# A chain of four conditional layers on one core: scores once, by query, and probabilities turned by a transposing DMA

## The chip, the cores and the metric

One core of one Trainium2 chip. Its engines are TensorE (PE, matmuls), VectorE (DVE), ScalarE (ACT), GpSimd (POOL) and SyncE (SP, which here only issues DMAs). Each engine runs its own list of instructions in order; semaphores tie the lists together. The metric is the time on the device in microseconds (us), lower is better.

## The reference

Sixteen independent batch elements, each x of 256 tokens by 256 features in float32, go through four layers, each added to its input:

```python
x = x + einsum('bnh,boh->bno', x, W[subject]) + b[subject]        # a linear layer chosen per element
x = x + zX*laplace_x(x) + zY*laplace_y(x) + zR*x*(1-x)            # a stencil
# attention: 16 heads of 16; query = side + b_self, keys = x + b_prev (masked by length) and one
# further score per query, its own: s_self = q . k(side); softmax over 256 + 1 scores
x = x + (softmax([q k^T, s_self] * SCALE) @ [v ; v_self]) @ Wo + bo
# three experts, relu(x @ wi) @ wo with hidden 1024: one chosen by label and two shared,
# mixed by a softmax gate that is computed from token 0
x = x + eo*w0 + s0*w1 + s1*w2
```

The attention's numbers have to be near float32, so the kernel splits operands into parts: float32 products are made of three matmuls (hi*hi, hi*lo, lo*hi), and query and key heads are laid out as bfloat16 bands (three parts each, six products, stacked to 96 rows, with the mask as one row more).

## The kernel before

Everything of one element fits in the on-chip memory; the loop runs over elements. Five written order lists (PE_BODY, ACT_BODY, DVE_BODY, POOL_BODY, SP_BODY) say in which order each engine makes the stages of one turn. A turn works on three elements at once: `lag(name)` gives 0 for the preparation of element i (x1, q, lap, kp, vp and so on), 1 for the attention of element i-1, 2 for the experts (H0 to H11, P0 to P11) and the gate of element i-2. Lists with OPEN_ in front stand ahead of the loop, those with CLOSE_ behind it; the loop makes 14 turns. In the opening there are no experts yet, and PE makes matmuls without use (`fill`) between stages; the opening's lists name 132 of them, the closing's list 5.

**Experts.** H_s (line 859) makes 256 hidden columns in one PSUM bank out of 12 matmuls, each 128x128 by 256 columns. ACT takes relu into `hid_hi` (1160), DVE the rest into `hid_lo` (1391); P_s (886) multiplies on into two output banks. Two hidden banks and two buffers alternate.

**Preparation.** x1, q, ks, vs, kp, vp are the same sort of 12-matmul product into one of two front banks. All users of the front banks take them in turns (`RING`, `open_bank` at 752): a stage waits until the user two places before it is freed. q and k parts are rewritten by SP into `q_rows` and `k_rows` (`place`, 527: 6 DMAs each, those of `kp` at 589 and `k3` at 601), which the scores of the next turn read.

**Attention of one head h, before.** S_h (826): two matmuls give scores with the query on the partitions; DVE reduces them to their maximum (1294) and frees the bank. After heads 0 to 7 and 8 to 15, `top0` and `top1` (1295) take the larger of that and the own score, and split it into three bfloat16 parts; `m0` and `m1` turn these on PE (835), ACT copies them to SBUF (1102), and SP writes them as three further rows of `q_rows` (604). E_h (841) then makes the scores a second time, with the key on the partitions and the maximum already subtracted by these rows; ACT makes two exps of 512 columns out of PSUM, one in float32 and one in float16 (1117, 1121; head 11's float16 one is a cast on DVE, 1313), DVE (seven heads) or POOL (nine heads) subtracts them into `prob_lo` (1314, 1607). `attend` (780) multiplies both parts with the values, eight matmuls of 49 columns, three heads behind E_h and between its two matmuls. Heads 0 to 7 fill `pv` first; `half` (1316) sums them, and POOL's `norm` (1593) divides. `att` (1328) does the same for heads 8 to 15 on DVE, after which PE turns the result (`aT`, 912) and multiplies by Wo. `m1` on POOL (1588) weighs the own values by `p_self`.

**Queues.** SP issues, in the order of SP_BODY, the pieces of the chosen expert's weights (`wo0`.., `wi_load`), the placements, the next element's inputs (`load`) and the store (`sum`). Each waits at the head of the queue for what it needs.

## Time and profile before

| | |
|---|---|
| Median of 3 runs (lowest to highest) | 1002.27 us (998.57 to 1002.36) |
| Profiled execution: its own time, its span | 998.3 us, 995.7 us |
| TensorE clock granted, mean | 0.997 |
| PE busy | 972.3 us, 98% of the span, 9659 matmuls |
| DVE, ACT, POOL busy | 796.9 (80%), 686.8 (69%), 635.9 us (64%) |
| DMA | 82.71 MB, 28% of 16 engines |
| Chain that ended last | PE 75%, POOL 9%, issue 8% |

Busy time is the union over an engine's instructions. PE's matmuls overlap each other, so the duration of one (about 0.28 us) is more than what it costs; the cost is the distance from its start to the next start. The chain view follows the last instruction back to what released it.

### The profile page before, as it was taken

What the parts mean: (1) busy time and instruction counts of PE and PEld (TensorE: products, weight loads), DVE (VectorE), ACT (ScalarE), POOL (GpSimd) and SP (SyncE); (2) the same over time, 40 slices, a digit from 0 to 9 for tenths busy, and PEclk for the clock granted to TensorE, in tenths of its full rate; (3) what the DMA queues carried; (4) which work ended last, traced back from release to release, by engine and by line L of the source; (5) the groups of instructions that cost most, each with busy time, mean ns of one, the idle gap of its engine ahead of it and who ended that gap; (6) DMA issues with size and microseconds to landing.
All of it is one profiled execution on the core that took longest, in us unless ns stands there. A gap on an engine that the chain in (4) does not pass through costs nothing.

```text
span 995.7 us, 28043 instructions
## 1 busy us (share of the span) xinstructions
PE 972.3 (98%) x9659; PEld 932.9 (94%) x9659; DVE 796.9 (80%) x1566; ACT 686.8 (69%) x1442; POOL 635.9 (64%) x544
## 2 busy tenths in 40 slices
PE   7889999999999999999999999999999999999997
...
DMA packets 92029, 82.71 MB, mean 83 GB/s; under 512 B 12100, under 2 KB 90980, under 8 KB 92004
## 3 DMA queue, kind: packets, MB, share of 16 engines
q1 hardware_dynamic: 91572, 81.99, 28.2%
q10 hardware_dynamic: 432, 0.39, 0.1%
q8 instruction: 15, 0.25, 0.1%
...
## 4 chain that ended last, share of the span: by engine, by line
PE 75%; POOL 9%; issue 8%; DVE 3%; ACT 3%; SPq 1%; DMA 1%; POOLq 0%; ACTq 0%; DVEq 0%
PE out L721 8%; PE out L722 8%; PE hid L721 8%; PE out L723 8%; PE hid L722 7%; PE hid L723 7%; PE front L847 4%; PE front L833 4%; PE front L721 4%; PE front L723 3%; PE front L722 3%; POOL prob_lo L1607 3%; POOL exp_lo L1543 2%; PE pv L788 2%; PE pv L789 2%
## 5 line engine op out<-in xcount | busy, mean ns | idle before, releaser
L721 PE MATMUL hid<-x_hi,exp_hi 128*128 128x256 f32 x768 | 230.6, 300 | 0.2
L721 PE MATMUL out<-hid_hi,exp_hi 128*128 128x256 f32 x768 | 229.0, 298 | 0.0
L1607 POOL TENSOR_TENSOR prob_lo<-prob,prob_hi 128x512 f16<-128x512 f32 x141 | 182.6, 1296 | 61.5 <-ACT prob_hi L1121 61.4
L722 PE MATMUL out<-hid_lo,exp_hi 128*128 128x256 f32 x768 | 217.3, 283 | 0.0
L723 PE MATMUL out<-hid_hi,exp_lo 128*128 128x256 f32 x768 | 216.8, 282 | 0.0
L722 PE MATMUL hid<-x_lo,exp_hi 128*128 128x256 f32 x768 | 216.5, 282 | 0.0
L723 PE MATMUL hid<-x_hi,exp_lo 128*128 128x256 f32 x768 | 216.2, 282 | 0.0
L1294 DVE TENSOR_REDUCE s_max<-front 128x2 f32<-128x512 f32 x247 | 163.5, 688 | 60.8 <-PE front L833 58.8
L1543 POOL TENSOR_TENSOR exp_lo<-raw,exp_hi 128x512 fp32r<-128x512 f32 x128 | 168.8, 1334 | 60.1 <-ACT exp_hi L1138 60.0
L1160 ACT ACTIVATE hid_hi<-hid 128x512 fp32r<-128x512 f32 x192 | 115.7, 603 | 101.2 <-PE hid L723 100.0
L1117 ACT ACTIVATE prob<-front 128x512 f32<-128x512 f32 x246 | 148.6, 604 | 24.2 <-PE front L847 20.6
L721 PEld LDWEIGHTS out<-hid_hi,exp_hi 128*128 128x128 f32 x768 | 146.2, 190 | 2.0 <-DVE hid_lo L1391 0.2
L1391 DVE SCALAR_TENSOR_TENSOR hid_lo<-hid,hid_hi 128x512 fp32r<-128x512 f32 x192 | 131.1, 683 | 21.1 <-ACT hid_hi L1160 20.1
L721 PEld LDWEIGHTS hid<-x_hi,exp_hi 128*128 128x128 f32 x768 | 144.9, 189 | 1.7 <-DVE x_lo L1378 0.5
L722 PEld LDWEIGHTS out<-hid_lo,exp_hi 128*128 128x128 f32 x768 | 146.5, 191 | 0.0
L723 PEld LDWEIGHTS out<-hid_hi,exp_lo 128*128 128x128 f32 x768 | 146.2, 190 | 0.0
L722 PEld LDWEIGHTS hid<-x_lo,exp_hi 128*128 128x128 f32 x768 | 145.5, 189 | 0.0
L723 PEld LDWEIGHTS hid<-x_hi,exp_lo 128*128 128x128 f32 x768 | 144.7, 188 | 0.0
L1121 ACT ACTIVATE prob_hi<-front 128x512 f16<-128x512 f32 x230 | 139.3, 606 | 0.0
L847 PE MATMUL front<-q_rows,k_rows 100*128 100x256 bf16 x492 | 117.8, 276 | 0.6 <-DMA q_rows<-max_rows 0.5
L1314 DVE TENSOR_TENSOR prob_lo<-prob,prob_hi 128x512 f16<-128x512 f32 x115 | 104.7, 911 | 16.7 <-ACT prob_hi L1121 15.6
L788 PE MATMUL pv<-v_cols,prob_hi 128*128 128x49 bf16 x1024 | 83.0, 185 | 3.8 <-DVE prob_lo L1314 2.7
...
## 6 DMA issues: line engine op xcount, KB each, us to landing
raw<-in_wi SPq DMA_DIRECT2D x64, 256.0 KB, 3.8
raw<-in_wo SPq DMA_DIRECT2D x64, 256.0 KB, 2.7
q_rows<-w_raw SPq DMA_DIRECT2D x80, 128.0 KB, 2.4
k_rows<-x_raw SPq DMA_DIRECT2D x48, 128.0 KB, 2.4
k_rows<-x1T SPq DMA_DIRECT2D x45, 128.0 KB, 2.3
x_raw<-in_x SPq DMA_DIRECT2D x16, 256.0 KB, 3.1
w_raw<-in_w SPq DMA_DIRECT2D x16, 256.0 KB, 2.7
s_raw<-in_side SPq DMA_DIRECT2D x16, 256.0 KB, 3.4
```

The source lines that it names most:

```text
L721: nc.tensor.matmul(acc, w_hi, a_hi, start=first, stop=False)
L722: nc.tensor.matmul(acc, w_hi, a_lo, start=False, stop=False)
L723: return nc.tensor.matmul(acc, w_lo, a_hi, start=False, stop=last)
L847: last = nc.tensor.matmul(psum[:, k * S:(k + 1) * S], k_rows[0:ROWS_EXP, h, k * P:(k + 1) * P], q_rows[0:ROWS_EXP, h, :], start=True, stop ...
L1117: last = nc.scalar.activation(prob[:, h % NPROB, :], psum[:, :], ACT.Exp, scale=SCALE)
L1121: last = nc.scalar.activation(prob_hi[:, h % NPROB, :], psum[:, :], ACT.Exp, scale=SCALE)
L1160: nc.scalar.activation(hid_hi[:, s % 2, :], hid_bank[s % 2][:, :], ACT.Relu).then_inc(hid_hi_done, 1)
L1294: nc.vector.tensor_reduce(s_max[:, :, h:h + 1], psum, AX_X, ALU.max).then_inc(freed["S"], 1)
L1314: nc.vector.tensor_tensor(prob_lo[:, h % NPROB, :], prob[:, h % NPROB, :], prob_hi[:, h % NPROB, :], ALU.subtract).then_inc(prob_split_dve, 1)
L1391: nc.vector.scalar_tensor_tensor(hid_lo[:, s % 2, :], hid_bank[s % 2][:, :], 0.0, hid_hi[:, s % 2, :].bitcast(F32), ALU.max, ALU.subtract) ...
L1543: nc.gpsimd.tensor_tensor(lo, source, hi.bitcast(F32), ALU.subtract).then_inc(w_split, 1)
L1607: nc.gpsimd.tensor_tensor(prob_lo[:, h % NPROB, :], prob[:, h % NPROB, :], prob_hi[:, h % NPROB, :], ALU.subtract).then_inc(prob_split_poo ...
```

## The change

Scores are made once, with the query on the partitions. SCALE moves into q (ACT's `q` and the query's bias). Per head: S_h on PE; DVE reduces to the negated maximum; ACT makes two exps of 256 columns, one for each half of the queries, with that maximum as the bias per partition, into `prob` (two buffers); ACT copies `prob` to float16 (new stage C_h, three buffers `prob_parts`); DVE or POOL subtracts to the low part; SP issues one DMA with transpose=True for both parts (new stage T_h), 128 partitions by 1024 float16, into one of three buffers `turned`, the third of which lies on ksT; PE multiplies with the values in a stage V_h. E_h's matmuls, m0, m1, the maxima's parts and their DMAs are gone. The maximum no longer contains the own score: `own0` and `own1` make from d = own - max the weights exp(min(d, 0)) and exp(min(d, 0) - d), and `half`, `norm` and `att` multiply the sums by the second, c_prev, before adding the own value. LO_DVE is now heads 1, 3, 5, 7, 9, 11, 13. gate_h lies on a `prob` buffer. `ks` on ACT waits for the last value matmul, as ksT is a buffer of turned probabilities; the placement of q waits for S15. All order lists are new; the opening's now name 190 fill matmuls, the closing's 5. The core of the diff:

```diff
 PE_BODY = """
-H0 H1 S0 S1 P0 S2 S3 H2 S4 S5 P1 S6 S7 H3 S8 P2 m0 H4 S9 S10 P3 S11 H5
-E0 S12 P4 E1 S13 H6 E2 S14 P5 E3 S15 H7 E4 E5 P6 E6 H8 m1 E7
-x1 P7 q E8 H9 E9 lap P8 E10 E11 H10 E12 kp E13 P9 E14 E15 H11 P10 pvend P11
-vs aT ks gate wo logits vp self
+H0 H1 S0 S1 P0 H2 S2 P1 S3 H3 S4 P2 H4 S5 S6 V0 P3 H5 S7 V1 V2 P4 x1 S8 V3 H6 P5 S9 V4 S10 H7 V5 V6 q S11 P6 S12 V7 H8 P7 S13 S14 V8 V9
+H9 H10 S15 V10 P8 lap V11 V12 P9 H11 kp P10 V13 V14 V15 P11 vs aT ks gate wo logits vp self
 ACT_BODY = """
+H0 x_parts w_parts H1 E0 E1 C0 C1 H2 wi0 E2 wi1 C2 wi2 H3 E3 E4 C3 s_parts H4 C4 E5 P3 C5 E6 H5 E7 C6 wi3 wo0 C7 E8 H6 C8 react E9 own0
+C9 E10 H7 wo1 q C10 x1_parts E11 x3_keep E12 C11 C12 H8 wo2 E13 P7 H9 qa C13 E14 C14 E15 C15 x2_parts wo3 H10 own1 qb H11 kp kq P11 aT
+ks vs logits x3_parts vp sum x2b
 DVE_BODY = """
+H0 S0 S1 H1 S2 H2 E1 S3 S4 x_parts H3 E3 S5 H4 S6 S7 E5 gate0a H5 S8 own0 x1 E7 S9 S10 H6 E9 H7 S11 S12 x1_parts half E11 S13 H8 S14
+react S15 E13 H9 lap own1 x2_parts H10 gate0b H11 gate1 kp att gate2 aT k3 relu wo logits mix x3_parts scale self vp
 POOL_BODY = """
+E0 x_parts wi0 E2 w_parts s_parts E4 wi1 wi2 E6 E8 wi3 wo0 wo1 E10 x1 E12 wo2 qa E14 E15 wo3 own norm qb ks sum vp
 SP_BODY = """
-wo0 wo1 m0 wo2 wo3 m1 wi_load E15 kp k3 load sum
+T0 T1 T2 T3 wo0 T4 T5 T6 wo1 T7 T8 T9 wo2 T10 T11 T12 wo3 T13 T14 T15 kp k3 load wi_load sum
...
-NPROB = 3
+NPROB = 2
+NPARTS = 3
+NTURNED = 3
...
+        def wait_turned(eng, i, h):
+            per_turn = len(range(h % NPARTS, H, NPARTS))
+            wait(eng, turned_in[h % NPARTS], 16 * per_turn, i, 16 * (h // NPARTS + 1))
...
+                elif name[0] == "T":
+                    h = int(name[1:])
+                    wait_prob_split(sp, i, h)
+                    sp.sem_inc(parts_seen, 1)
+                    if h == NTURNED - 1:
+                        wait_filled(sp, i, "self")
+                        sp.sem_inc(self_seen, 1)
+                    wait(sp, pv_done, H, i, max(h - NTURNED + 1, 0))
+                    sp.sem_inc(values_seen, 1)
+                    sp.dma_start(turned[h % NTURNED], prob_parts[:, h % NPARTS].rearrange("p n t -> p (n t)"), transpose=True).then_inc(turned_in[h % NPARTS], 16)
                 elif name == "kp":
+                    wait_filled(sp, i - 1, f"S{H - 1}")
...
             def attend(i, h):
-                wait_prob_split(pe, i, h)
+                wait_turned(pe, i, h)
...
                     for k in range(C):
-                        at = k * S + t * P
-                        nc.tensor.matmul(acc, prob_hi[:, h % NPROB, at:at + P], v_cols[:, k, h, :], start=(k == 0), stop=False)
-                        last = nc.tensor.matmul(acc, prob_lo[:, h % NPROB, at:at + P], v_cols[:, k, h, :],
-                                                start=False, stop=(k == C - 1))
+                        hi, lo = (turned[h % NTURNED][:, n * C * C + t * C + k, :] for n in range(2))
+                        nc.tensor.matmul(acc, hi, v_cols[:, k, h, :], start=(k == 0), stop=False)
+                        last = nc.tensor.matmul(acc, lo, v_cols[:, k, h, :], start=False, stop=(k == C - 1))
...
                 elif name[0] == "E":
                     h = int(name[1:])
-                    wait_filled(act, i, name)
+                    wait(act, max_done, H, i, h + 1)
                     if h >= NPROB:
                         wait_prob_split(act, i, h - NPROB)
-                    psum = front_psum(name, i)
-                    last = nc.scalar.activation(prob[:, h % NPROB, :], psum[:, :], ACT.Exp, scale=SCALE)
-                    if h not in HI_DVE:
-                        if h >= NPROB:
-                            wait(act, pv_done, H, i, h - NPROB + 1)
-                        last = nc.scalar.activation(prob_hi[:, h % NPROB, :], psum[:, :], ACT.Exp, scale=SCALE)
-                    last.then_inc(freed["E"], 1)
+                    psum = chunked(front_psum(f"S{h}", i))
+                    for t in range(C):
+                        last = nc.scalar.activation(prob[:, h % NPROB, t * S:(t + 1) * S], psum[:, t, :], ACT.Exp, bias=neg_max[:, t, h:h + 1])
+                    last.then_inc(freed["S"], 1)
+                elif name[0] == "C":
+                    h = int(name[1:])
+                    wait_freed(act, i, f"S{h}")
+                    wait_turned(act, i, h - NPARTS)
+                    nc.scalar.activation(prob_parts[:, h % NPARTS, 0, :], prob[:, h % NPROB, :], ACT.Copy).then_inc(hi_done, 1)
...
-                    nc.vector.tensor_reduce(s_max[:, :, h:h + 1], psum, AX_X, ALU.max).then_inc(freed["S"], 1)
+                    nc.vector.tensor_reduce(neg_max[:, :, h:h + 1], psum, AX_X, ALU.max, negate=True).then_inc(max_done, 1)
...
+                    linkf(nc.vector.scalar_tensor_tensor(d, s_self[:, :, heads], 1.0, neg_max[:, :, heads], ALU.mult, ALU.add))
+                    nc.vector.tensor_scalar(p_self[:, :, heads], d, 0.0, None, ALU.min)
+                    nc.vector.scalar_tensor_tensor(c_prev[:, :, heads], d, 0.0, d, ALU.min, ALU.subtract).then_inc(d_self_done, 1)
...
+                    weighted = of_step(nc.vector.tensor_tensor(den[:, :, heads], sums[:, :, :, 3 * DH], c_prev[:, :, heads], ALU.mult))
...
+                        summed[t] = of_step(nc.vector.tensor_tensor(by_head(t), by_head(t), spread(c_prev, t), ALU.mult))
...
+                    for t in range(C):
+                        by_head = att[:, t, cols].rearrange("p (h d) -> p h d", d=DH)
+                        nc.gpsimd.tensor_tensor(by_head, by_head, c_prev[:, t, 0:HALF].unsqueeze(2).to_broadcast([P, HALF, DH]),
+                                                ALU.mult).then_inc(norm_link, 1)
```

## Rows read from the trace of the kernel before

**Rows 1.** Busy time by engine (and instructions), clock, DMA share, GB/s, by stretch.
```profile
481.08:540.19 59.11, 58.87 (x594) 56.79 (x593) 48.84 (x97) 42.15 (x89) 38.99 (x33) 1.00 0.27 80
28.00:64.00 36.00, 31.02 (x329) 26.83 (x330) 30.86 (x57) 25.07 (x51) 27.47 (x24) 0.95 0.39 119
```

**Rows 2.** PE in order of time: start, duration, engine, line, out<-in, count.
```profile
481.08 0.63 PE L749 MATMUL pv<-ident,att 128*128 128x128 f32 x4
...
499.82 0.28 PE L839 MATMUL front<-ident_half,m_parts 128*128 128x128 bf16 x2
...
500.12 0.28 PE L722 MATMUL hid<-x_lo,exp_hi 128*128 128x256 f32 x1
500.24 0.28 PE L723 MATMUL hid<-x_hi,exp_lo 128*128 128x256 f32 x1
...
504.98 0.39 PE L847 MATMUL front<-q_rows,k_rows 100*128 100x256 bf16 x2
505.20 0.38 PE L833 MATMUL front<-k_rows,q_rows 97*128 97x256 bf16 x2
...
510.81 0.19 PE L788 MATMUL pv<-v_cols,prob_hi 128*128 128x49 bf16 x1
...
511.02 0.27 PE L847 MATMUL front<-q_rows,k_rows 100*128 100x256 bf16 x1
```

**Rows 3.** ACT in order of time.
```profile
509.43 0.59 ACT L1117 ACTIVATE prob<-front 128x512 f32<-128x512 f32 x1
509.91 0.60 ACT L1121 ACTIVATE prob_hi<-front 128x512 f16<-128x512 f32 x1
...
540.86 0.84 ACT L1152 ACTIVATE ak_hi<-pv,vec_sb 128x256 fp32r<-128x256 f32 x2 [1.23 <-PE pv L749]
541.59 0.60 ACT L1090 ACTIVATE v_self<-front 128x512 f32<-128x512 f32 x1
```

**Rows 4.** Groups by line and form: busy us, mean ns | idle before, releaser.
```profile
L1607 POOL TENSOR_TENSOR prob_lo<-prob,prob_hi 128x512 f16<-128x512 f32 x141 | 182.6, 1296 | 61.5 <-ACT prob_hi L1121 61.4
...
L1601 POOL TENSOR_TENSOR att<-att,den 128x128 f32<-128x128 f32 x32 | 20.2, 651 | 1.3
...
L1313 DVE CAST prob_hi<-prob 128x512 f16<-128x512 f32 x16 | 16.3, 1017 | 3.6 <-PE pv L789 3.6
...
L749 PE MATMUL pv<-ident,att 128*128 128x128 f32 x64 | 10.1, 280 | 1.3 <-DVE att L1344 1.3
...
L1066 ACT ACTIVATE w_raw<-q_full 128x512 bf16<-128x512 f32 x16 | 9.9, 616 | 0.1
```

**Rows 5.** DVE in order of time, around top0 and top1.
```profile
498.02 0.84 DVE L1301 SCALAR_TENSOR_TENSOR s_max<-s_max,s_self 128x16 f32<-128x16 f32 x1
...
499.58 0.69 DVE L1294 TENSOR_REDUCE s_max<-front 128x2 f32<-128x512 f32 x1
...
513.58 1.26 DVE L1301 SCALAR_TENSOR_TENSOR s_max<-s_max,s_self 128x16 f32<-128x16 f32 x1
...
516.48 0.68 DVE L1391 SCALAR_TENSOR_TENSOR hid_lo<-hid,hid_hi 128x512 fp32r<-128x512 f32 x1
```

**Rows 6.** DVE in order of time, first and last instructions of att.
```profile
478.35 0.17 DVE L1334 TENSOR_TENSOR den<-pv,p_self 128x16 f32<-128x16 f32 x1 [0.74 <-PE pv L789]
...
480.50 0.49 DVE L1344 TENSOR_TENSOR att<-att,den 128x128 f32<-128x128 f32 x2
```

**Rows 7.** DMA queue of SP on the page: packets, MB, share of 16 engines.
```profile
q1 hardware_dynamic: 91572, 81.99, 28.2%
```

**Rows 8.** SP's DMA issues in order of time: start, duration, count.
```profile
486.08 0.37 SPq L539 DMA_DIRECT2D x_raw<-in_x  x1
...
533.85 3.86 SPq L531 DMA_DIRECT2D q_rows<-w_raw  x5
...
544.12 0.40 SPq L549 DMA_DIRECT2D w_raw<-in_w  x1
```

**Rows 9.** DMA issues on the page: count, KB each, us to landing.
```profile
q_rows<-w_raw SPq DMA_DIRECT2D x80, 128.0 KB, 2.4
...
out<-e_out SPq DMA_DIRECT2D x16, 256.0 KB, 2.2
```

247 lines of the change are left out of this document (104 added, 143 removed).

## The prediction

> **What bounds the kernel now.** I read the busy time by stretches first. In the steady loop, between the transposes of one batch's attention and the next batch's, 59.11 us pass, and TensorE (PE) is busy in 58.87 of them at a granted clock of 1.00 [rows 1]. VectorE (DVE) works 48.84 us, ScalarE (ACT) 42.15, GpSimd (POOL) 38.99 of the same 59.11, and the DMA engines 0.27 of it. The opening (28 to 64 us, 31.0 of 36 busy) leaves PE idle; the closing stretch I take as the loop. The reader is to see that one engine is full and no other is above 83%, so a microsecond of PE instructions taken out of a batch is worth up to a microsecond, times 14 loop turns and about one more in the closing stretch, until another engine, a queue or a latency takes over.
>
> Then I read PE in order of time, for the price of each kind of work as the distance between starts (durations overlap, as matmuls are pipelined). An E stage (two 256-column matmuls) starts at 504.98 and the next stage at 505.20: 0.22 us [rows 2]. The eight value matmuls of one head start at 510.81 and the next matmul at 511.02: 0.21 us. An m stage (two 128-column transposes) and the matmul behind it reach from 499.82 to 500.12, of which one ordinary pitch is 0.12, so it costs 0.18.
>
> **What the change takes from PE.** Scores by key (E0 to E15) go: 16 x 0.22 = 3.5 us a batch. m0 and m1 go: 2 x 0.18 = 0.4. The value matmuls stay at 8 a head with the same shapes, now in stages V0 to V15 of their own instead of between an E's two matmuls; 16 x 0.21 as before. Together -3.9 us a batch, from 59.1 to 55.2. The transposes cost PE nothing, as they are made by DMA. The bounds on this term are 3.5 (if small gaps at new stage borders eat 0.4) and 4.3.
>
> **ACT.** Before, a head is two 512-wide exps; starts 509.43 and 509.91, so 0.48 each [rows 3]; 31 of them are 14.9 us. After, a head is two 256-wide exps with a bias per partition and one 512-wide copy to float16 out of SBUF. The nearest row to such a pair is the biased pair out of PSUM at 540.86, behind which the next starts at 541.59: 0.73. The copy is nearest to the bf16 one of 616 ns [rows 4], less the 0.12 by which neighbours overlap: 0.50. So 16 x (0.73 + 0.50) = 19.7, that is +4.8, and ACT stands at 42.15 + 4.8 = 47.0 us, 85% of 55.2; the two copies of the maxima's rows go as well and are not counted. Bounds: if each exp costs the bf16 copy's 0.50 it is 24 us, +9.1, which gives 51.3, still under 55.2. Nothing else hides this; it is paid in slack alone.
>
> **DVE.** The maxima's split goes: 498.02 to 499.58 and 513.58 to 516.48, 4.5 us a batch [rows 5]; in its place two own steps of three small instructions, about half of the shorter one each, 0.8 (2.9 each at worst). Head 11's cast goes, 1.0 [rows 4]. "half" and "att" gain a weighting by c_prev: one multiply and one add on the sums (0.2 each) and, in "att", two multiplies over 128x128 (about 0.25 each) [rows 6], some 1.1 together. Net about -3.4, to 45.4 us (82%). Seven of the 16 subtractions remain on it.
>
> **POOL.** Still nine subtractions; "norm" gains two multiplies of 651 ns [rows 4], 1.3 us, to 40.3 (73%). It has cover, except in the stretch ahead of aT: there "own" and "norm" now stand behind E15 and wo3, and what is late is PE's aT.
>
> **What is late next.** Before aT, PE has P11 and vs (24 matmuls, 2.9 us) behind the last value matmul, while DVE needs from 478.35 to 480.99 for "att" [rows 6]; PE started its transposes 0.09 us later and sat idle 1.3 us for it over the whole run [rows 4]. "att" is thus exactly as long as its cover. The new one has a multiply and three more small steps, its waits interleaved: I take +0.5 us (bounds 0.3 and 1.1), all of it PE waiting, once a batch. The second source is the front PSUM pair: a score bank is now released only after DVE's maximum, both exps and whatever ACT has queued ahead (before, the scores' bank went free after the 0.7 us maximum and E's after two exps); S of two heads on waits for that, and behind it queue H and P, which have nothing to do with attention. ACT at 85% instead of 71% makes such waits likelier. I take another 0.5 us a batch (0 to 2). Together 1.0, and a turn of 56.2 us.
>
> **The transposing DMA.** 16 a batch, 256 KB each, all issued by SP, between the wo loads and ahead of kp, k3, load, wi_load. No transposing DMA is in this trace, so three prices are needed.
> Bandwidth: the queue moved 81.99 MB in 28.2% of 16 engines' 995.7 us, 292 GB/s [rows 7]; 16 x 0.26 MB at that is 14.4 us, which with 0.27 x 59.1 = 16.0 fills 30 of 55 us. At half the rate it is 45 of 55, still under.
> Issue on SP: a plain 256 KB load takes 0.37 us, a placement of 128 KB in 256 pieces 3.86 / 5 = 0.77 [rows 8]. A transposed head lands in 128 partitions x 8 blocks, 1024 runs of 256 bytes; if issue goes by pieces it is 4 x 0.77 = 3.1 us. SP's other 27 DMAs of a turn, from the first to the last shown and without the two m placements, come to 16.4 us of issue. At 0.37 SP holds 22 us, at 3.1 it holds 66. SP is full at (55.2 - 16.4) / 16 = 2.4 us an issue, and the kernel loses from (59.1 - 16.4) / 16 = 2.7 us. I take about 1.6, the middle of the two ends, for 42 us: hidden, though what is behind T15 (the placements for the next batch) starts later. Before, the last of them was out ahead of the w load at 544.12, and S0 still has vp, H0 and H1 of PE in front of it, 36 x 0.12 = 4.3 us, which is the cover.
> Landing: 2.2 us (a store) to 2.4 (a placement) + 3 x 0.77 = 4.7 us [rows 9]. Head h may be sent once V(h-3) is done and its subtraction is in; V(h) stands about 10 us of PE work behind S(h), and maximum, exps, copy and a POOL subtraction take 0.7 + 0.8 + 0.6 + 1.3 = 3.4 [rows 3 to 5]. So 4.7 fits in the 6.6 left. Three buffers at 3.45 us a head give 10 us per buffer.
> The Trainium skill (Advanced Engine Details and Errata, X-Bar Transpose) says that on trn2 a transposing DMA is as fast as a regular one; no run here shows it yet, and it would keep the sum as it is. It also speaks against the change (VectorE: DVE Perf Modes, The three transpose paths): 1309 ns for one 128x128 bf16 block by DMA, which for eight blocks in a row would be an estimated 10.5 us a head and 168 us a batch, some 2500 us in all.
>
> **The sum.** Profiled execution before: 995.7 us span, 2.6 around it, 998.3 in all; the median of the runs, 1002.3, lies 0.4% above. Loop: 14 x (3.9 - 1.0) = -40.6. Closing: the same stages go from batch 15, 3.9 less the same 1.0, -3. Opening: PE is not full there; the fill matmuls go from 132 to 190, 58 x 0.12 = +7.0 (counted in the order lists of the diff), E and m go, -3.9, and ACT gains 4.8 in a stretch where it is busy 25 of 36: +3. 998.3 - 40.6 - 3 + 3 = 957.7; I say **958 us**. With no new waits it is 944, with 2.6 us a turn 981.
>
> **Rivals.**
> *A, the gain is eaten by in-order waits (12%).* ACT at 85% and DVE at 82% both serve H (hid_hi, hid_lo) and S. If PE cannot be kept full once ACT passes about 80%, a turn is 47.0 / 0.8 = 58.7, 0.4 less than before, and the time about 992 (985 to 1000). For: ACT waits in front of H and E now, so it has little order left to trade. Against: DVE was at 83% and PE full. Half of this case is within 0.5%.
> *B, SP's queue becomes the bound (17%), slower.* At 3.1 us an issue a turn is 16 x 3.1 + 16.4 = 66 us: 998 + 14 x 6.9 + some 6 in the opening = about 1100. It decides from 2.7 us an issue; between 2.4 and 2.7 it only eats gain. For: placements, the nearest transfers by pieces, cost nearly twice as much for half the bytes. Against: a placement gathers from two dimensions, and nothing shows that issue grows with pieces beyond that. PE would then wait at V, with H and P behind it.
> *C, transposes run one after the other (4%), slower.* If a transpose must land before the next starts and takes the 4.7 us, a turn is 16 x 4.7 = 75 us and the time about 1225. The Trainium skill's 1309 ns a block would be this case, further out.
> *Forecast (67%), PE still the bound*; its own range is 938 to 985.
>
> **How the numbers follow.** A difference of 0.5% is about what a measurement of this kernel can tell from none. Faster by more: 0.67 + 0.06 = 0.73. Within: 0.06 of A less a little, 0.05. Slower: B and C and the rest, 0.22. The range that holds 8 in 10 runs from 936 to 1030: below lies only a turn under 55.0 us, above most of B and C.
>
> **What would show it.** PE busy over 97% of a turn of 55 to 57 us, the E and m groups gone, value matmuls at the same 0.02 to 0.03 us pitch. ACT near 47 us a turn, an exp of 256 at about 0.47 us of duration. PE's idle ahead of the attention's transposes grown from 0.1 to some 0.5 us a turn. The transposing DMA's issue on SP at 1 to 2.4 us and landing under 5. The forecast is wrong if SP is issuing nearly all the time or PE's waits are at V on the DMA (B, C), or if PE's waits at S and H add up to 3 us a turn (A).

## The result, and the profile after

The changed kernel takes **983.62 us** (median of 4 runs, 982.84 to 985.09), the kernel before 1001.49 on the same chip (998.57 to 1002.36): ratio 0.9828, 95% interval 0.9804 to 0.9853. The forecast was 958 us and 43 us of gain; 18 came. The profiled execution took 982.84 us with a span of 981.0.

Where the rest went is read from one event per batch, the start of the transposes of the attention (aT, L749). S0 is the first score matmul, V0 and V15 the first and last start of batch 0's value matmuls; a turn is the distance from one aT to the next, in the last column the mean of the 13 turns from the second aT to the fifteenth.

```
us in the span      S0    V0   V15  V0-V15   aT 1   aT 2  aT 15  aT 16    end   turn
before            28.5  41.6  63.6    22.0   67.4  126.4  894.9  947.3  995.7  59.12
after             32.6  42.0  78.5    36.5   82.2  144.0  876.0  929.6  981.0  56.31
```

Until the first aT the new kernel loses 14.8 us, in the first turn 2.8 more (61.8 against 59.0); 13 turns give back 36.5; from the fifteenth aT to the end it loses 4.2 (105.0 against 100.8). The sum is -14.7. The side of before rests on one profile.

A turn of the loop, with the engines' busy times as in [rows 1] (PE, weight load, DVE, ACT, POOL, clock, DMA share, GB/s), and under it the opening's stretch of value matmuls:
```profile
425.50:482.00 56.50, 55.11 (x557) 53.49 (x557) 47.33 (x94) 45.89 (x104) 38.51 (x35) 1.00 0.69 158
42.00:78.50 36.50, 26.94 (x284) 24.68 (x283) 23.92 (x42) 24.90 (x56) 14.71 (x14) 0.91 0.84 156
```
The same heads in the kernel before, which the sum in the prediction did not look at by itself:
```profile
41.60:63.60 22.00, 17.97 (x234) 15.50 (x232) 19.55 (x34) 18.62 (x38) 16.36 (x14) 1.00 0.26 82
```
In the loop PE is at 97.5%. In the opening none of the four computing engines reaches 75% any more (before, DVE was at 89% and ACT at 85%). The DMA engines do: their share went from 0.26 to 0.84. Whether they set the pace is taken up with the experiments.

Groups of PE and ACT by line and form, as in [rows 4]:
```profile
L749 PE MATMUL pv<-ident,att 128*128 128x128 f32 x64 | 11.0, 296 | 17.4 <-DVE att L1337 17.4
L1091 ACT ACTIVATE prob<-front,neg_max 128x256 f32<-128x256 f32 x494 | 206.2, 478 | 31.6 <-DVE prob_parts L1287 22.4 <-POOL prob_parts L1606 4.5 <-DVE neg_max L1275 0.3
L1097 ACT ACTIVATE prob_parts<-prob 128x512 f16<-128x512 f32 x256 | 160.0, 639 | 14.2 <-DMA turned_own<-prob_parts 6.2 <-DMA ksT<-prob_parts 5.1
```
The transposing DMA by its source line (its issue on SP in ns, minimum, median, maximum, and the landing):
```profile
L591 SPq DMA_TRANSPOSE turned_own<-prob_parts x176: 1231/1252/2382, 37.5 to 923.0; - x176
L591 SPq DMA_TRANSPOSE ksT<-prob_parts x80: 1231/1237/2604, 43.1 to 921.6; - x80
...
DMA to landing us min/median/max: 3.0/3.2/5.7
```
Its queue on the page, as in [rows 7]:
```profile
q1 hardware_dynamic: 361044, 148.74, 67.1%
```
PE waits 17.4 us ahead of aT where it waited 1.3 [rows 4]. 3.5 of the 17.4 are in batch 0, and so are all of the 1.3: in the loop before, PE never waited there, where the prediction had spread the 1.3 over the turns as 0.1 each. The queue's share is up from 28.2 to 67.1%.

How long a head takes shows in the chain of the critical work for the last head of the opening (start, us, what): exponential, copy, subtraction, the DMA with 3.05 us from the start of its issue to its landing, and then att, 3.5 us with PE idle. "Landing" is counted from the start of the issue everywhere here, so the 1.25 us of issue lie inside the 3.2.
```profile
72.50 0.47 ACT x1T L1057
72.97 0.73 ACT prob L1091 x2
73.70 0.12 ACT own_w L1083
73.81 0.56 ACT prob_parts L1097
74.39 0.70 DVE prob_parts L1287
...
75.20 0.05 issue
75.24 3.05 DMA turned_own<-prob_parts
78.29 0.05 issue
...
78.76 0.18 DVE den L1321
...
81.69 0.49 DVE att L1337 x2
```

In the closing, PE's waits from the fifteenth aT to 945 (us in total, times, longest):
```profile
PE pv L749 <- DVE att L1337: 2.1, 2, 1.1
PE front L831 <- ACT prob L1091: 1.9, 2, 1.4
PE pv L721 <- DVE ak_lo L1347: 1.5, 1, 1.5
```
And busy times by stretch; the 12 us behind the last aT have a granted clock of 0.86:
```profile
876.00:929.90 53.90, 49.97 (x506) 47.33 (x507) 39.80 (x84) 39.70 (x90) 27.86 (x26) 1.00 0.79 155
929.90:942.00 12.10, 9.45 (x64) 8.83 (x62) 4.45 (x11) 3.39 (x7) 1.27 (x1) 0.86 0.10 27
```

### The profile page after: what moved, and what is told of

Same layout as the page of the kernel before. It is cut to its first block, busy times and chain, and to the rows that moved or that the text cites. A ratio compares the mean times of both kernels' runs of the same rounds, so it can differ in the third digit from the quotient of the medians.

```text
span 981.0 us, 28407 instructions
## 1 busy us (share of the span) xinstructions
PE 926.3 (94%) x9141; PEld 894.5 (91%) x9141; DVE 776.6 (79%) x1518; ACT 748.7 (76%) x1682; POOL 624.6 (64%) x576
## 3 DMA queue, kind: packets, MB, share of 16 engines
q1 hardware_dynamic: 361044, 148.74, 67.1%
## 4 chain that ended last, share of the span: by engine, by line
PE 40%; DVE 20%; issue 17%; POOL 7%; ACT 6%; DMA 5%; SPq 4%; DVEq 0%; ACTq 0%; POOLq 0%
PE hid L721 4%; PE hid L722 4%; PE hid L723 4%; PE out L721 4%; PE out L722 4%; PE out L723 4%; DVE neg_max L1275 3%; DVE gate_terms L1400 3%; PE front L831 3%; DVE prob_parts L1287 3%; DMA turned_own<-prob_parts 2%; PE front L721 2%; ACT prob L1091 2%; PE front L723 2%; PE front L722 2%
## 5 line engine op out<-in xcount | busy, mean ns | idle before, releaser
L1606 POOL TENSOR_TENSOR prob_parts<-prob,prob_parts 128x512 f16<-128x512 f32 x141 | 164.8, 1169 | 135.5 <-ACT prob_parts L1097 135.0
L1091 ACT ACTIVATE prob<-front,neg_max 128x256 f32<-128x256 f32 x494 | 206.2, 478 | 31.6 <-DVE prob_parts L1287 22.4
L721 PE MATMUL hid<-x_hi,exp_hi 128*128 128x256 f32 x768 | 224.6, 292 | 1.2 <-DVE hid_lo L1384 1.2
L1275 DVE TENSOR_REDUCE neg_max<-front 128x2 f32<-128x512 f32 x247 | 166.9, 687 | 60.7 <-PE front L831 57.5
L722 PE MATMUL out<-hid_lo,exp_hi 128*128 128x256 f32 x768 | 214.2, 279 | 0.0
L1537 POOL TENSOR_TENSOR exp_lo<-raw,exp_hi 128x512 fp32r<-128x512 f32 x128 | 180.3, 1422 | 41.1 <-ACT exp_hi L1113 41.0
L1097 ACT ACTIVATE prob_parts<-prob 128x512 f16<-128x512 f32 x256 | 160.0, 639 | 14.2 <-DMA turned_own<-prob_parts 6.2
L722 PEld LDWEIGHTS out<-hid_lo,exp_hi 128*128 128x128 f32 x768 | 144.7, 188 | 0.0
L1287 DVE TENSOR_TENSOR prob_parts<-prob,prob_parts 128x512 f16<-128x512 f32 x115 | 116.8, 1016 | 28.4 <-ACT prob_parts L1097 28.4
L831 PE MATMUL front<-k_rows,q_rows 97*128 97x256 bf16 x494 | 89.3, 278 | 3.6 <-ACT prob L1091 2.3
L1113 ACT ACTIVATE exp_hi<-raw 128x512 fp32r<-128x512 f32 x128 | 80.0, 639 | 7.2 <-DMA raw<-in_wo 6.6
```

Source lines behind the costliest of these rows:

```text
L721: nc.tensor.matmul(acc, w_hi, a_hi, start=first, stop=False)
L722: nc.tensor.matmul(acc, w_hi, a_lo, start=False, stop=False)
L831: last = nc.tensor.matmul(psum[:, t * S:(t + 1) * S], q_rows[0:ROWS_MAX, h, t * P:(t + 1) * P], k_rows[0:ROWS_MAX, h, :], start=True, stop ...
L1091: last = nc.scalar.activation(prob[:, h % NPROB, t * S:(t + 1) * S], psum[:, t, :], ACT.Exp, bias=neg_max[:, t, h:h + 1])
L1097: nc.scalar.activation(prob_parts[:, h % NPARTS, 0, :], prob[:, h % NPROB, :], ACT.Copy).then_inc(hi_done, 1)
L1275: nc.vector.tensor_reduce(neg_max[:, :, h:h + 1], psum, AX_X, ALU.max, negate=True).then_inc(max_done, 1)
```

## The experiments

Each ratio is to the kernel before on the same chip; the changed kernel's own is 0.9828. Five kernels (after, e7, e8, e12, e14) have the same opening. Their profiles tell how far one profile can be read: V0 to V15 36.5 to 38.3 us, S0 at 32.6 to 35.7, first aT at 82.2 to 86.5. So in the opening V0 to V15 is compared (mean of the five 37.4), and less than 2 us of it counts for nothing. From aT 15 to the end, the closings with nothing changed in them take 103.4 to 106.2 us (14 profiles, e3 and e9 left out, mean 104.6). All read in the same way:

```
                    S0    V0   V15  V0-V15   aT 1   aT 2   aT 15   aT 16     end   turn
e1_plain          34.4  44.1  76.9    32.8   81.1  140.6   862.3   913.7   964.7  55.52
e2_sp_open        28.4  41.3  76.3    35.0   80.0  142.0   874.3   928.3   978.4  56.33
e3_scores_twice   34.3  46.1  82.5    36.4   85.6  150.4   917.2   972.7  1023.8  58.98
e4_no_fills       32.7  40.8  77.0    36.2   80.1  140.3   873.3   927.1   978.5  56.38
e5_loads          34.1  43.4  77.7    34.3   81.0  143.2   876.1   929.3   979.5  56.38
e6_open_all       28.5  38.9  75.0    36.1   77.8  140.4   873.4   926.7   976.9  56.38
e7_close          34.1  44.1  80.9    36.8   84.7  146.4   879.2   931.5   981.8  56.37
e8_den            35.7  45.5  83.8    38.3   86.5  148.2   880.7   934.8   985.0  56.35
e9_two_parts      32.5  41.3  82.0    40.7   85.7  158.0  1019.9  1084.6  1134.8  66.30
e10_open_alone    34.0  43.6  75.7    32.1   78.7  153.8   887.6   940.6   991.7  56.45
e11_open_fills    30.1  40.0  75.2    35.2   78.0  139.9   872.9   927.2   977.4  56.38
e12_pool_hold     34.3  44.0  81.0    37.0   83.8  144.8   877.1   931.9   983.3  56.33
e13_five_parts    31.7  41.6  77.3    35.7   80.1  142.9   875.6   929.7   980.8  56.36
e14_pool_qb       34.0  43.9  82.1    38.2   84.9  145.8   879.1   932.5   983.9  56.41
e15_alone_five    32.5  41.9  72.8    30.9   76.3  150.1   882.8   936.1   987.5  56.36
e16_scores_ahead  29.8  39.8  77.3    37.5   80.5  141.5   873.4   926.7   977.7  56.30
e17_ahead_five    29.9  40.0  76.0    36.0   79.2  140.9   873.7   926.8   977.1  56.37
e18_alone_all     29.9  39.9  67.1    27.2   70.1  144.7   878.3   931.2   983.4  56.43
```

**e1_plain.** What does the transposing itself cost? The kernel computes something else; so that its sums stay finite, the exponential's scale and bias and the mask are changed as well.
```
-  sp.dma_start(turned[...], prob_parts[...], transpose=True)
+  sp.dma_start(turned[...], prob_parts[...])
...
-  nc.scalar.activation(..., ACT.Exp, bias=neg_max[...])
+  nc.scalar.activation(..., ACT.Exp, bias=ones[...], scale=0.001)
...
-MASKED = -1.0e30
+MASKED = 0.0
```


> Edit: the sixteen transposing DMAs of a batch become plain copies of the same 256 KB; so that sums stay finite the exponentials take the scale 0.001 and the bias 1, and the mask is 0: the probabilities and the output are other ones, waits and sizes are not. Theory (the transposing DMA sets the pace of the heads in the opening and holds up the closing turn, and is hidden in the loop): issue on SP 1.25 us falls well under 1, landing 3.1 us falls to about 2, DMA share of the loop falls from 0.69 to about 0.35; loop turn stays at 56.3 +- 0.3 us; in the opening the first attention turn (aT) comes at 74 to 77 us instead of 82.2, closing 1 us shorter, total 974 to 978 us (-6 to -10). Rival (engine order, probability buffers and the clock set the opening; the DMA is beside them): aT within 1.5 us of 82, total within 3 us of 983.6. Second rival (the DMA costs in the loop too, through its queue and the packets it takes): turn below 55.5 us and total below 970.

965.6 us, ratio 0.967 (0.9653 to 0.9688): 16.3 us of span less than after. Neither side had it. The opening gains 1.1 us until the first aT and the first turn 2.3, each of the 13 turns 0.79, together 10.3, and the rest 2.6. The issue takes 0.47 us for 1.25, the landing 2.3 us for 3.2 (0.8 of these 0.9 us are the issue), and the queue is busy 47.8% instead of 67.1 with the same megabytes. By source line, on the page, and a turn by stretch:
```profile
L591 SPq DMA_DIRECT2D turned_own<-prob_parts x176: 464/471/545, 39.3 to 906.2; - x176
```
```profile
q1 hardware_dynamic: 127572, 148.72, 47.8%
```
```profile
418.30:473.80 55.50, 54.70 (x557) 53.37 (x558) 46.55 (x94) 45.70 (x104) 38.46 (x35) 1.00 0.50 161
```
ACT is busy 45.7 us of a turn here and 45.9 in after, so the changed exponential costs the same. Where it stands in the loop, the distances between PE's starts tell: in the turn from 425.5 of after the start of P8 and that of lap are 1.82 us apart and here 1.50, lap takes 0.58 and 0.48, and P9 starts 0.46 and 0.02 behind V12's last value matmul. The waits show DVE's hid_lo as the releaser ahead of P9, 3.0 us in 13 turns, and none here. So about 16 of the missing 25 us are the price of a transposing against a plain transfer, spread over every stage.

**e2_sp_open and e5_loads.** SP's order in the opening; then the loads of shared pieces.
```
-mask shared2 k1 q0 q1 q2 mask_row k2       (e2)
+mask shared2 q0 q1 mask_row q2 k1 k2
-... T3 shared5 T4 ... T7 shared6 T8 ... T11 shared7 T12 ...   (e5; ACT's shared5 goes behind vs.1)
+... T15 shared5 shared6 shared7
```


> Edit: only SP's order in the opening: q0 q1 mask_row q2 k1 k2 as in the kernel before, instead of k1 q0 q1 q2 mask_row k2. Theory (k1, which waits for the keys' second part, holds up the placing of the queries that was ready at 18 us): the first scores start at 28.5 to 30 us instead of 32.6, all behind them moves with it, total -3 to -4 us (980 us). Rival (the heads' pace behind it is set by DMA engines that are full until 70 us, whenever the scores start): first scores earlier by 3 us or more, but aT at 81 to 82 us and total within 1 us of 983.6.

> Edit: in the opening the loads of the shared weights' pieces 5, 6 and 7 are issued behind the sixteenth transposing DMA instead of between the fourth and thirteenth, and ScalarE's copy of piece 5 goes behind them. Theory (these 512 KB loads share SP's queue and the 16 DMA engines with the transposing DMAs, whose landings of up to 5.7 us come right behind them): no landing above 3.5 us, aT 82.2 -> 78 to 80 us, first turn unchanged or 1 us longer, total -1 to -3 us. Rival (the heads' pace is set by ScalarE, VectorE and GpSimd, whatever the landing, as the plain copies of the last kernel suggest, whose aT came at 81.1): aT within 1 us of 82.2, total within 1.5 us of 983.

e2: 982.38 us, 0.985 (0.983 to 0.987). S0 comes 4.2 us earlier and V0 only 0.7: GpSimd is still at shared pieces until 34 us and starts head 0's subtraction at 36.5. e5: 981.83, 0.9846 (0.9819 to 0.9872); V0 to V15 34.3 us. The DMA of head 8, which stood right behind a shared piece and landed in 5.7 us, now lands in 3.5; elsewhere landings of up to 5.1 are left. Neither changes the time measurably.

**e3_scores_twice.** Is the loop bound by PE?
```
-for t in range(C):
+for t in (*range(C), *range(C)):     # the two score matmuls of a head, twice
```


> Edit: each head's two score matmuls are issued twice (the same result): 32 more matmuls a batch at 0.11 us, 3.5 us of TensorE a turn. Theory (the loop is bound by TensorE, 97.8% busy): turn 56.3 -> 59.8 us, total 983.6 + 14 x 3.5 + about 3 = 1034 to 1040 us. Rival (the turn is set by the chain exponential, copy, subtraction, transposing DMA, sums, and TensorE's matmuls are stretched beside it): turn below 58 us, total below 1010 us.

1023.4 us, 1.0255 (1.0226 to 1.0284): the turn grows by 2.67 us. The starts of two pairs behind each other in a turn of after stand 0.15 to 0.23 us apart, so 16 pairs are 2.4 to 3.7. PE's busy time in the 13 turns goes from 715.9 to 757.1 us, 3.2 a turn, and its waits from 15.2 to 9.9: a turn takes nearly all that PE is given, and the waits that were there take up some of the rest. That is less than the theory's 3.5 and far over the rival's bound.

**e4_no_fills, e6_open_all and e11_open_fills.** The opening's fills, then all opening edits at once without and with the fills.
```
-fill6 ... fill8 ... fill14 ... (120 filling matmuls behind S0)      (e4)
+(none)
 e6: e4, e2, e5, DVE "att shared4" for "shared4 att", POOL "vp E0 E2 shared3" for "shared3 vp E0 E2"
 e11: e6 with the fills kept
```


> Edit: all 120 filling matmuls of the opening behind the first scores are left out (98 of them ahead of the first aT, 18 behind wo; the 70 ahead of the scores stay). Theory (in the opening TensorE waits for the heads' chain, the fills lie in its waits): aT at 82 +- 1.5 us and total within 3 us of 983.6, with the granted clock of the opening lower, 0.5 to 0.7 on average, which may give a microsecond or two back the wrong way. Rival (the fills are in TensorE's queue ahead of work that is ready): 98 x 0.11 = 10.8 us less until aT, aT at 72 to 75 us, total 973 to 977 us.

> Edits, opening only: SP's order of the kernel before for the rows (q0 q1 mask_row q2 k1 k2); loads 5 to 7 behind the sixteenth transposing DMA; the 120 fills behind the first scores left out; VectorE's splitting of shared piece 4 behind att instead of ahead of it; GpSimd's splitting of shared piece 3 (2.7 us) behind the subtraction of head 2 instead of ahead of head 0. Theory (several covers of nearly equal length lie beside each other, so that each edit alone gives 2 us or less and all together more): aT 82.2 -> 70 to 74 us, first turn at most 61.8, total -8 to -12 us (971 to 975). Rival (a chain that none of the edits touches sets the pace: two probability buffers, exp, copy and subtraction in turn): aT at 77 to 80 us as with one edit, total -2 to -4 us.

> Edit: as the kernel with all opening edits, but with the 120 fills kept. Theory (without fills the granted clock of that stretch fell to 0.5 and the f32 products of batch 1 took twice as long, which ate what the other edits gave): V0 at 39 us, V0 to V15 33 to 34 us instead of 36, aT at 75 to 76 us, total -5 to -7 us against 983 (977). Rival (fills cost what they give): aT at 77.8 +- 1 us, total 979 +- 1.5.

e4: 982.22 us, 0.9848 (0.9833 to 0.9862); V0 to V15 stays at 36.2. With the fills their clock goes too (granted 0.61 in this stretch instead of 0.91), so what is shown is that the fills together with the clock that they hold up cost nothing. Of the 120, 102 stand ahead of aT. e6: 978.98, 0.9799 (0.9781 to 0.9817); e11: 978.89, 0.98 (0.9766 to 0.9834). First aT 4.2 to 4.4 us earlier, more of it in V0 than in the pace. In e6 the granted clock was 0.50 from 38.9 to 62 us, in e11 0.86 from 40.0 to 75.2, and the times are the same; the theory of e11 falls.

These stretches also tell whether the DMA engines or the clock set the pace of the opening. With the loads moved away the DMA share falls to 0.70 (e11) and 0.63 (e17), and V0 to V15 stays at 35.2 and 36.0; in e18 below it is 27.2 with a share of 0.82 and the clock at 0.50, the lowest of all. So neither sets it by itself.
```profile
40.00:75.20 35.20, 26.45 (x281) 23.72 (x282) 20.88 (x37) 23.43 (x53) 19.58 (x19) 0.86 0.70 124
40.00:76.00 36.00, 27.10 (x282) 24.79 (x282) 21.69 (x37) 23.15 (x53) 18.88 (x18) 0.82 0.63 109
```

**e7_close.** The closing order.
```
-... P9 V13 P10 V14 V15 P11 aT wo         ACT: H11 P11 aT
+... P9 V13 V14 V15 P10 aT P11 wo         ACT: H11 aT P11
```


> Edit: only the closing order: TensorE V13 V14 V15 P10 aT P11 wo instead of V13 P10 V14 V15 P11 aT wo; ScalarE's aT ahead of its P11. Theory (P11 behind aT covers the making of ak_hi and ak_lo as in the kernel before): the 1.48 us that wo waits goes, the waiting ahead of aT stays near 1.1, total -1.5 us. Rival (V15 now waits for the last transposing DMA that P10 covered): 1.2 to 1.5 us of waiting appear ahead of V14 and V15, total within 0.5 us.

From the fifteenth aT to the end 102.6 us instead of 105.0: the wait of 1.5 ahead of wo is gone, and the stretch behind aT runs at full clock; a V waits 0.6 for its DMA. PE's waits, and the stretch:
```profile
PE pv L749 <- DVE att L1337: 2.0, 2, 1.1
...
PE pv L788 <- DMA turned_own<-prob_parts: 0.6, 1, 0.6
```
```profile
931.80:943.80 12.00, 10.18 (x83) 9.69 (x82) 4.74 (x13) 4.06 (x10) 1.27 (x1) 1.00 0.16 51
```
The whole run does not show it (985.51 us, 0.9863, 0.9844 to 0.9882), as this run's unchanged opening ended 2.5 us later than after's. e17, with the same order, has 103.4, so against the mean of the unchanged closings the order is worth 1.2 to 2.0 us.

**e8_den, e12_pool_hold and e14_pool_qb.** The wait ahead of aT. In the loop of after, DVE's and GpSimd's instructions side by side:
```profile
478.49 0.16 DVE L1321 TENSOR_TENSOR den<-pv,own_w 128x16 f32<-128x16 f32 x1
478.57 1.01 DVE L1322 TENSOR_REDUCE att<-pv 128x128 f32<-128x384 f32 x2
479.50 1.13 DVE L1325 TENSOR_TENSOR den<-den,own_w 128x16 f32<-128x16 f32 x1
```
```profile
479.43 1.16 POOL L1565 TENSOR_TENSOR x1T<-s_raw,w_raw 128x512 bf16<-128x512 f32 x1
```
```
-den = tensor_tensor(den, p_self, add)                  (e8)
+den = scalar_tensor_tensor(den, 1.0, p_self, mult, add)
-POOL: own norm qb      +POOL: own norm (wait for att_done) qb     (e12)
-POOL: own norm qb      +POOL: own qb norm                         (e14)
```


> Edit: one instruction a turn, the sum den = den + p_self of heads 8 to 15 in VectorE's att (16 elements a partition), is written as scalar_tensor_tensor (x 1.0, + p_self) instead of tensor_tensor. In the trace of after it starts at 479.50 and ends at 480.63, as GpSimd's tensor_tensor of 479.43 to 480.59 ends; in the opening, with GpSimd idle, it takes 0.16. Theory (a tensor_tensor of VectorE with both operands in SBUF waits while GpSimd's instruction runs, the other form does not): the instruction 1.13 -> 0.17 us, the wait ahead of aT 0.93 -> under 0.1 us a turn, turn 56.4 -> 55.5, total -12 to -14 us (970). Rival (it waits for the result of the instruction ahead of it or for the memory, in any form): instruction and turn unchanged, total within 1 us. Second rival (the instruction is short, but what follows takes the wait over): turn within 0.3 us of 56.4.

> Edit, loop only: GpSimd waits for att_done ahead of qb (its subtraction q_rest - q_parts 1, which ran beside VectorE's att). The kernel before this one showed that VectorE's sum den + p_self takes 1.14 us in either form while GpSimd works. Theory (it waits for GpSimd's instruction to end): with GpSimd idle the sum takes 0.17 us, aT's wait of 0.93 us goes, turn 56.4 -> 55.5, total -12 us (971). Rival 1 (it is slow for another reason, such as the semaphore wait on the instruction two ahead): 1.13 us and 56.4 us unchanged. Rival 2 (qb later by 2.5 us delays the placing of q and k for the next batch and so its first scores): sum short, but the turn within 0.3 us of 56.4 or above.

> Edit, loop only: GpSimd's order own qb norm instead of own norm qb; it is never made to wait. Theory (VectorE's sum den + p_self waits for the GpSimd instruction that runs, and now meets ones of 0.4 us instead of one of 1.2): the sum 1.13 -> 0.2 to 0.5 us, the wait ahead of aT 0.93 -> 0.3 to 0.5 us or GpSimd's own last product for aT takes its place, turn 56.4 -> 55.9 to 56.1, total -3 to -6 us (978 to 980). Rival (the loop's turn is a ring through GpSimd, ScalarE and the score banks that takes 56.3 us however aT's wait goes, as with the held GpSimd): aT's wait falls and waits of about the same length appear ahead of the scores or of hid_lo, turn 56.3 to 56.4, total within 1.5 us of 983.

e8 (986.19 us, 0.9862, 0.984 to 0.9883): the form makes no difference.
```profile
L1325 DVE SCALAR_TENSOR_TENSOR den<-den,own_w x16: 163/1142/1145, 85.0 to 933.3; 128x16 f32<-128x16 f32 x16
```
e12 (984.49, 0.9852, 0.9831 to 0.9873): with GpSimd idle the sum takes 0.16 us in every batch, and PE never waits for att in the loop; but the turn is 56.33. PE now waits for the score banks instead. The sum by its source line (ns), and PE's waits from 150 to 876 us, of e12:
```profile
L1325 DVE TENSOR_TENSOR den<-den,own_w x16: 158/163/168, 82.3 to 930.4; 128x16 f32<-128x16 f32 x16
```
```profile
PE front L831 <- ACT prob L1091: 11.6, 24, 0.8
```
e14 (984.31, 0.9853, 0.9839 to 0.9867): the sum takes 0.37 us, as long as the GpSimd instruction it now meets, and still PE waits for att and the turn is 56.41. The same two of e14:
```profile
L1325 DVE TENSOR_TENSOR den<-den,own_w x16: 165/374/383, 83.4 to 931.0; 128x16 f32<-128x16 f32 x16
```
```profile
PE pv L749 <- DVE att L1337: 11.1, 12, 1.0
```
The 0.8 us that the sum gives back are lost a few instructions earlier. GpSimd's qb, moved ahead, now meets VectorE's product of the gate (L1400): the pair of them takes 1.78 us in e14 and 1.02 in after, and att starts 1.0 us behind the last value matmul instead of 0.3. So e14 only moves the loss along VectorE's list and says nothing about a ring behind it. After, and the two rows of e14 in the same place of the turn:
```profile
476.55 1.02 DVE L1400 SCALAR_TENSOR_TENSOR gate_terms<-gate,e_out,gate_terms 128x256 f32<-128x256 f32 x2
```
```profile
479.56 1.78 DVE L1400 SCALAR_TENSOR_TENSOR gate_terms<-gate,e_out,gate_terms 128x256 f32<-128x256 f32 x2
479.71 1.35 POOL L1565 TENSOR_TENSOR x1T<-s_raw,w_raw 128x512 bf16<-128x512 f32 x1
```
In e12 holding GpSimd back made it the next in line: the chain of its turn goes through its subtractions to ScalarE's exponential and the score banks:
```profile
445.58 1.21 POOL prob_parts L1608
447.04 0.15 issue
447.19 0.48 ACT prob L1091
447.71 0.39 PE front L831 x2
```
That a GpSimd held back this long closes such a ring behind PE is shown; whether there is one without the hold, and whether another order could have the short sum and no wait, isn't.

**e9, e10, e13, e15: the ring of part buffers.** The theory for the opening was that a buffer of f16 parts is busy for copy, subtraction, issue and landing, some 6.2 us, and there are three. That sum counts the issue twice: copy 0.6, subtraction 0.7 to 1.2 and 3.1 from the start of the issue are at most 4.9.
```
-NPARTS = 3      +NPARTS = 2                                                      (e9)
 e10: all stages x.1 of the opening behind V15 on PE, behind C15 on ACT, att on DVE, norm on POOL
-parts: h % 3    +parts: h % 5 for batch 0 (two in free ends of gate1 and e_out)  (e13, on e11)
 e15: e10, e5 and e13's five buffers
```


> Edit: two buffers of f16 parts instead of three (the copy of head h now waits for the transposing DMA of head h-2 instead of h-3). Theory (the heads' pace in the opening is a ring: copy 0.6 us, subtraction 0.7 to 1.2, issue 1.25, landing 3.1, then the copy that reuses the buffer, some 6.2 us for as many heads as there are buffers): with three buffers 2.1 us a head at best, with two 3.1; first to last sum (V0 to V15) in the opening 36.5 -> 46 to 50 us. In the loop, where a head comes every 3.5 us, the turn stays below 58.5 us. Rival (batch 1's front stages between the heads set the pace): V0 to V15 36.5 -> at most 41 us.

> Edit, opening only: all stages of batch 1 (splits, x1, react, lap, q, kp, ks, vs) go behind batch 0's sixteen heads on every engine instead of between them. The kernel is expected to be slower as a whole; what counts is V0 to V15 of batch 0. Theory (the ring of part buffers): V0 to V15 36.5 -> 31 to 33 us, 2.1 us a head. Rival (batch 1's stages between the heads set it): V0 to V15 falls to 24 us or less, 1.6 us a head, the pace of ScalarE's exponential, copy and nothing else.

> Edit: the kernel with all opening edits and the fills, and beside them five buffers of f16 parts instead of three for batch 0 alone (two lie in parts of gate1 and e_out that are free until then; the load of shared piece 5 waits for them). Theory (the opening's pace is a ring: copy, subtraction, issue, landing, some 6.4 us for as many heads as there are part buffers, so 2.1 us a head with three): with five the ring allows 1.3 us a head and the next limit (two probability buffers, 1.5 us a head; three turned buffers, 1.5) sets it: V0 to V15 35.2 -> 27 to 30 us, aT 78.0 -> 70 to 73, total 979 -> 971 to 974. Rival (batch 1's stages between the heads set it by waits of one engine for another, and the ring only comes second): V0 to V15 33 to 35 us, total 977 to 979.

> Edit: batch 1's stages behind batch 0's sixteen heads (as in the kernel that did this alone, V0 to V15 32.1 us), loads 5 to 7 behind the sixteenth transposing DMA, and five buffers of parts for batch 0. Slower as a whole; V0 to V15 counts. Theory (ring of part buffers): 32.1 -> 23 to 26 us, 1.5 to 1.7 us a head. Rival (landing and issue of the transposing DMA one behind the other on SP, or the engines' own pace, set 2.1 us a head whatever the buffers): 30 us or more.

Two buffers: 1139.02 us, 1.1397 (1.1362 to 1.1431); V0 to V15 40.7, the rival's figure, and a turn of 66.3, far over the 58.5 expected. In the loop ScalarE now waits for landings ahead of its copy, 137.6 us in 13 turns, where it waited 1.6 in after:
```profile
ACT prob_parts L1097 <- DMA turned_own<-prob_parts: 137.6, 91, 2.7
```
Batch 1 out of the way: 32.1, where the ring theory had it (993.49 us, 0.9931, 0.9907 to 0.9956). Five buffers: 35.7, against 35.2 without (979.03 us, 0.9799, 0.9784 to 0.9815). Five and batch 1 away: 30.9, the rival's side (990.65 us, 0.9921, 0.9903 to 0.994). The theory falls: three buffers are enough, two would have been the slower case.

**e16, e17, e18: the written orders.** 
```
 PE  -S6 S7 V0 S8 V1 S9 V2 V3 .. V4 .. V5 S10 S11 S12 .. V6 .. S13 V7 S14 S15 V8
     +S6 S7 S8 V0 S9 V1 S10 V2 S11 V3 .. S12 V4 .. S13 V5 .. S14 V6 .. S15 V7 V8     (e16, on e11)
 ACT -E7 own0 x1_parts.1 E8 C7   +E7 own0 C7 E8 x1_parts.1                           (e17, with e13, e7)
 ... e16 moves DVE's maxima of heads 10 to 15 as much, e17 also DVE's x1.1 two places later
 e18: e15 and e2, PE's order of e16, POOL's shared3 as in e6, no fills behind V0, DVE "E11 half" for "E9 half"
```


> Edit: the kernel with the opening edits and the fills, and in its opening TensorE's scores of heads 8 to 15 are written two to four places earlier (S8 ahead of V0, S9 ahead of V1, ... S15 ahead of V7, instead of S10 behind V5 and S15 behind V8), VectorE's maxima of heads 10 to 15 as much earlier. Theory (what sets the pace is TensorE's written order: S10 stands behind V5, which waits for the transposing DMA of head 5, so a ring of V5, S10, maximum, exponential, copy, subtraction, issue, landing, V10 takes 10 us for five heads, 2.1 a head, and more buffers or a shorter landing shorten only a part of it): V0 to V15 35.2 -> 28 to 31 us, aT 78 -> 71 to 74, total 979 -> 972 to 976. Rival (several rings of near 2.1 us a head, the three part buffers the next): V0 to V15 33 to 35 us and total 978 to 980, and only together with five buffers does it fall.

> Edits: the last kernel, and with it five buffers of parts for batch 0, ScalarE's copy of head 7 and exponential of head 8 ahead of batch 1's x1_parts (which waits for VectorE's x1), and the closing order V13 V14 V15 P10 aT P11 wo. Theory (nested rings: scores behind sums, three buffers, one engine's wait for batch 1): V0 to V15 35.2 -> 24 to 27 us, aT 67 to 70, closing 2.4 us shorter, total 966 to 970. Rival (the pace is ScalarE's, VectorE's and GpSimd's own work with two probability buffers and batch 1 between): V0 to V15 31 us or more, total 974 to 977.

> Edit, opening only: batch 1's stages behind batch 0's heads, five buffers of parts, loads 5 to 7 behind, SP's order of before for the rows, and with these TensorE's scores two to four places earlier, no fills behind V0, and VectorE's half (which waits for V7) behind its subtraction of head 11 instead of head 9. Slower as a whole than the others; V0 to V15 of batch 0 counts (30.9 us with the first three). Theory (the pace is the sum of many places where an in-order engine waits for a sum or a transposing DMA that another engine's order holds back; none alone is worth more than 3 us, all gone leave two probability buffers, exp 0.85, copy 0.6, subtraction 0.7 to 1.2 for two heads): V0 to V15 22 to 26 us, 1.5 to 1.7 a head. Rival (issue of 1.25 us and landing of 3.1 us with three turned buffers hold 2 us a head whatever the orders): 29 us or more.

e16: V0 to V15 37.5, no gain (981.01 us, 0.9825, 0.9801 to 0.9849). e17: 36.0 (980.43, 0.9804, 0.978 to 0.9828). e18: 27.2 (984.51, 0.9852, 0.9815 to 0.989), between its two expectations and near the lower, so its rival and e15's, that issue and landing hold 2 us a head whatever the orders, are out; S0 to aT 40.2 us against 49.6 in after and 38.9 before. The stretch of e18, in which still no computing engine is above 68%:
```profile
39.90:67.10 27.20, 10.99 (x140) 7.37 (x141) 14.72 (x26) 18.47 (x43) 14.17 (x16) 0.50 0.82 144
```
The gain is paid back by batch 1, whose stages come later: the second aT of e18 is at 144.7, of after at 144.0. Of the 17 kernels that compute the reference (e1 does not) none beats the changed one by more than the intervals tell; the best (e6, e11, e13) lie at 0.98.

## Why the forecast was wrong, step by step

The profile before and after differ by 14.7 us where the sum had some 41. By stage: until the first aT 14.8 lost instead of 3, in the first turn 2.8 lost instead of 2.9 won, in the 13 turns 36.5 won instead of 37.7, behind them 4.2 lost instead of 3 won; 11.8 + 5.7 + 1.2 + 7.2 = 26 us too little.

**PE's term and the turn: right.** Forecast 55.2 us of PE work and 1.0 of new waits, a turn of 56.2; measured 56.31. With plain copies, which take one cause of waits away, it is 55.52 with 0.8 still ahead of aT (10.4 us in 13 turns). The place of the waits was only partly right: 0.9 ahead of aT (0.5 said), 0.2 ahead of P9 for hid_lo, and almost none at the score banks (0.5 said). That their sum came out at 1.2 for 1.0 with one nearly twice as large and the other absent is luck. The 13 turns gave 36.5 us, 2.8 each for 2.9 in the sum.

**ACT, DVE, POOL: near.** ACT 45.9 us (47.0 said), POOL 38.5 (40.3), DVE 47.3 (45.4). DVE's miss of 1.9 is in what its instructions meet, not in their number. The seven subtractions take 1052 ns each in the loop after, 954 with plain copies and 926 before, 0.9 us a turn; the sum in att takes 1.13 instead of the 0.2 said; and react, x_lo and the terms of z, which are the same instructions as before, went from 0.68, 0.63 and 0.17 us to 1.44, 1.24 and 0.93.

**The transposing DMA: inside the bounds, and not free.** Issue 1.25 us (1.6 taken), landing 3.2 with the issue in it (2.2 to 4.7), DMA busy 0.69 of the turn, 39 us (30 at the rate of before, 45 at half of it). Rivals B and C fall: SP issues 16 x 1.25 = 20 us for them in a turn, and a turn is not 66 or 75. But "hidden" was the wrong word: against a plain transfer it costs 0.8 us a turn and some 6 us in the two ends. The queue's time rose from 28.2% of 995.7 us to 67.1% of 981.0, by 377 us for 67 MB, an estimate of 178 GB/s; with the plain copy it is 47.8% of 964.7, 180 us more than before, 372 GB/s. The Trainium skill (Advanced Engine Details and Errata, X-Bar Transpose) has transposing DMAs as fast as regular ones; this case's traces do not agree: it is half the rate, 2.7 times the issue, and 0.9 us more until the landing, of which 0.8 are the longer issue. Its 1309 ns a block (VectorE: DVE Perf Modes, The three transpose paths), eight in a row, does not add up either: a head of eight blocks and 128 rows lands in 3.2 us.

**The opening: the step that failed.** "+3" was a sum of busy times: fills +7.0, E and m -3.9, ACT's in slack; the latency of the DMA in each head stood in it at nothing. Measured to the first aT +14.8, and the first turn, which the sum had at -2.9, came at +2.8. The fills, the only term of size in it, are not it: of the 58 more, 34 stand ahead of the first scores, 18 behind aT and only 6 between, and without them V0 to V15 is 36.2 instead of 36.5 and the time the same (e4). What is there instead is length. A head used to go exponentials, subtraction, sum; now it goes exponential, copy, subtraction, DMA 3.2 us from issue to landing, sum. In the loop a head has 3.5 us to itself and PE has the experts' work between. In the opening PE has little else, and each engine's written order has a place where it waits for a sum, for a buffer or for batch 1: heads come every 2.4 us instead of every 1.5, with no computing engine above 75%. The runs show what it isn't, taken one at a time: not the fills (e4), not the loads between the DMAs beyond 2 to 3 us (e5), not the number of part buffers (e13), not PE's scores behind its sums (e16), not the share of the DMA engines (e11, e17) nor the clock (e18). The three turned buffers make SP wait 1.4 us in these 36; the two probability buffers were in no experiment. Plain copies and batch 1's stages are worth some 4 to 5 each (e1, e10). Only all together give 9 to 10 (e18). So what is shown is that orders, part buffers and loads together, with the same DMA, hold 9 to 10 of the 14 us, and that a shorter DMA in the old orders gives 4 to 5; that the two are one cause, the latency of a head in orders that leave it no room, is the reading that fits both. A split of the 14 us on single waits isn't shown, and e18 does not separate which of its additions to e15 gave the last 3.7.

**The closing: wrong in sign.** -3 forecast, +4.2 measured (+3.8 with the mean of the unchanged closings, 104.6). 1.2 to 2.0 of it is an order: P11 ahead of aT instead of behind, so that wo waits 1.5 us for ak_lo, and the clock is 0.86 in the 12 us behind it (e7: 1.00 and no wait). Plain copies give 2.2 to 2.6 there. The remaining waits are, among others, those of the score banks for ScalarE (1.9) and of aT for att (1.1 in batch 15). The fills have no part in it: the closing names 11 of them in both kernels, not 5. The prediction took the closing "as the loop"; it is a turn without the other batch's front, so the head has less work beside it. That this is why the rest is lost, as in the opening, is argued and not shown.

Rival A (992) names in-order waits in the loop, and these were as forecast. It was right about the kind of loss and wrong about the place.

Three sums of the prediction are slightly off and change nothing: with no new waits it comes to 943 us and not 944, the four terms of DVE add up to -3.6 and not -3.4, and 168 us in each of 16 batches are some 2700 and not 2500.
